# A fused attention and feed-forward kernel: the last head group gets its own tables, and GpSimd takes over the weight split and two row copies

## What is computed

```python
def attn(x, w_attn, w_proj, adapter_wte, gating):        # x is (2, 1024, 512), 32 heads of 16
    q, k, v = split(x @ w_attn.T)                        # q and k then get a rotary embedding
    y = softmax(causal(q @ k.T / sqrt(16))) @ v          # per head
    y = y + gating * softmax(q @ ak.T / sqrt(512)) @ av  # 10 adapter rows, no mask
    return y @ w_proj.T

def ffn(x, base_w, base_b, A, B, router_w):              # 16 experts of rank 64, top 2
    combine = top2(softmax(x @ router_w.T))
    return x @ base_w.T + base_b + 0.5 * einsum(combine, x @ A.T, B)

x = layernorm(x + attn(x, ...))
x = layernorm(x + ffn(x, ...))
```

## Time and profile before

| | us |
|---|---|
| median of three runs | 926.55 |
| lowest and highest of them | 924.72, 932.81 |
| time of the profiled execution | 920.5 |
| its span, first to last instruction | 918.8 |
| PE busy in it | 872.9 (95%) |
| DVE, ACT, POOL busy | 727.6, 471.5, 233.6 |

### The profile page before, as it was taken

One profiled execution on the slowest core, in us unless ns is written; L12 is line 12 of the kernel. 1 busy time (PEld: TensorE's weight loads), 2 busy tenths in 40 slices (PEclk: granted clock), 3 DMA queues, 4 the chain that ended last, 5 costly groups with the idle time before them and its releaser, 6 DMA issues.

```text
span 918.8 us, 15954 instructions
## 1 busy us (share of the span) xinstructions
PE 872.9 (95%) x5420; PEld 565.5 (62%) x5420; DVE 727.6 (79%) x2224; ACT 471.5 (51%) x1036; POOL 233.6 (25%) x269
## 2 busy tenths in 40 slices
PE   5999999988999999999999999999989999999995
PEld 4778787664444444444444444443468888888884
DVE  4675757776889999999999999996477777777766
ACT  4232323111488888888888888887651221212110
POOL 0212121201223332333333323234242222121211
PEclk9999999996599999999999999999999999999999
DMA  7225253604532233333322233333010010101010
GB/s 258 92 69 161 70 161 93 165 18 120 115 60 53 43 61 70 72 71 71 72 48 51 48 70 72 71 102 106 11 36 24 24 46 23 46 23 46 24 36 34
DMA packets 31825, 65.03 MB, mean 71 GB/s; under 512 B 5580, under 2 KB 7052, under 8 KB 31756
## 3 DMA queue, kind: packets, MB, share of 16 engines
q1 hardware_dynamic: 31244, 62.58, 26.3%
q10 hardware_dynamic: 512, 1.57, 0.9%
HBM read 42.54 MB, written 20.97 MB: 69 GB/s over the span
## 4 chain that ended last, share of the span: by engine, by line
PE 81%; DVE 12%; ACT 3%; issue 2%; POOL 1%; DMA 1%; SPq 0%; DVEq 0%; ACTq 0%; POOLq 0%
PE bank L1372 16%; PE bank L1273 16%; PE bank L1283 12%; PE bank L351 10%; PE bank L353 10%; PE bank L352 10%; PE bank L1473 3%; PE bank L1354 2%; DVE xl L814 1%; DVE xtl L1000 1%; ACT xth L757 1%; DVE asb L874 1%; DVE asum L877 1%; ACT asb L640 1%; DVE asum L872 1%
## 5 line engine op out<-in xcount | busy, mean ns | idle before, releaser
L732 ACT ACTIVATE pt<-bank 128x512 f32<-128x512 f32 (+3 forms) x768 | 325.2, 495 | 71.9 <-PE bank L1273 65.5
L896 DVE CUSTOM_DVE_ANT_0 bank<-bank,cmask 128x512 f32<-128x512 f32 (+3 forms) x512 | 234.4, 527 | 12.1 <-PE bank L1283 9.1
L1273 PE MATMUL bank<-qs,ks 50*128 50x512 f32 (+3 forms) x768 | 221.8, 404 | 1.7 <-ACT pt L732 1.3
L1273 PEld LDWEIGHTS bank<-qs,ks 50*128 50x128 f32 x768 | 113.1, 189 | 141.5 <-ACT pt L732 124.4
L1283 PE MATMUL bank<-ks,qs 48*128 48x512 f32 (+3 forms) x768 | 172.3, 402 | 9.0 <-DVE mx L896 6.0
L899 DVE TENSOR_REDUCE mx<-bank 128x1 f32<-128x512 f32 x256 | 161.1, 688 | 14.8 <-PE bank L1283 13.0
L1372 PE MATMUL bank<-pt,vb 128*32 128x512 f32 (+3 forms) x1536 | 167.2, 508 | 0.7 <-POOL pt L570 0.7
L570 POOL TENSOR_SCALAR_AFFINE_SELECT pt<-pt 128x512 f32<-128x512 f32 x128 | 83.4, 651 | 290.3 <-ACT pt L732 290.3
L1283 PEld LDWEIGHTS bank<-ks,qs 48*128 48x128 f32 x768 | 96.0, 194 | 42.8 <-DVE mx L896 16.5
L521 POOL TENSOR_TENSOR part<-rope,part 128x1024 fp32r<-128x1024 f32 x16 | 38.2, 2389 | 190.3 <-ACT part L631 190.3
L757 ACT CAST xth<-bank 128x512 fp32r<-128x512 f32 x16 | 9.4, 586 | 141.4 <-PE bank L1447 141.4
(11 more groups left out here) (149 smaller groups left out, 1405.4 us busy)
## 6 DMA issues: line engine op xcount, KB each, us to landing
q_parts<-part SPq DMA_DIRECT2D x32, 256.0 KB, 3.0
k_parts<-part SPq DMA_DIRECT2D x32, 256.0 KB, 3.2
qs<-q_parts SPq DMA_DIRECT2D x30, 256.0 KB, 4.0
ks<-k_parts SPq DMA_DIRECT2D x30, 256.0 KB, 6.8
vb<-in_x SPq DMA_DIRECT2D x16, 256.0 KB, 2.6
out<-outb SPq DMA_DIRECT2D x16, 256.0 KB, 2.0
qs<-q_parts SPq DMA_DIRECT2D x30, 128.0 KB, 5.0
ks<-k_parts SPq DMA_DIRECT2D x30, 128.0 KB, 5.8
```

The lines of the kernel that those rows point to most:

```text
L732: act.activation(pt[k % PT_BUFS][:, h, 0:width(st)], half(n % SCORE_BUFS)[:, 0:width(st)], ACT.Exp, scale=float(HD) ** -0.5).then_inc(S("e ...
L896: last = ve.tensor_tensor_reduce(blk, blk, cmask[:, BANK - nk * P:], 1.0, NEG, ALU.add, ALU.max, mx[m][:, 0, h, qt:qt + 1])
L1273: pe.matmul(half(n % SCORE_BUFS)[:, 0:q1 - q0], ks[g % 3][r0:r0 + KX, h // 2, kb * P:(kb + 1) * P], qs[g % 3][r0:r0 + KX, h // 2, q0:q1], ...
```

## The change

- Group 15 has tables of its own. Its `weighted` steps are put beside chunks 15, 21, 27, 31, 36, 39, 41, 42, 45, and three after the last chunk; its first half is copied at 32; the transposes go to chunks 13 and 39.
- `t_y(0)` goes from chunk 5 to chunk 0, `t_y(1)` stays at 7. The eight projection pieces go from chunks 11, 12, 15, 16, 21, 24, 25, 29 to 6, 12, 19, 20, 25, 29, 33, 35.
- POOL's two row copies go from the start of group 15 to the start of group 14.
- The projection's weight is loaded in group 11 and split by POOL in group 12, in four pieces of 128x512 (a copy and a subtraction each), ahead of the masks of steps 1 to 3 and after the mask of step 3. DVE has no split(0) any more.
- DVE's order becomes hi_y(0), lo_y(0), hi_y(1), lo_y(1), invert(14, 1), split(1), norms(0, 0), norms(1, 1), invert(15, 0).
- POOL's `normalise(14, 1)` comes after the mask of step 3 in group 15, and `normalise(15, 0)` after all masks of group 15.

```diff
+LAST_VALUES_AT = [15, 21, 27, 31, 36, 39, 41, 42, 45, 48, 49, 50]
+LAST_COPY_AT = [32, 58]
+LAST_NORM_CHUNK = [13, 39]
...
-Y_AT = [5, 7]
-PROJ_AT = [(11, 12, 15, 16), (21, 24, 25, 29)]
+Y_AT = [0, 7]
+PROJ_AT = [(6, 12, 19, 20), (25, 29, 33, 35)]
+SPLIT_GROUP = G - 4
...
+                if g == SPLIT_GROUP - 1:
+                    sp.wait_ge(S("v_built"), GB)
+                    load_weight(0)
                 if g == G - 2:
-                    sp.wait_ge(S("v_built"), GB)
-                    for n in range(2):
-                        load_weight(n)
+                    load_weight(1)
...
+            def split_proj(c_):
+                gp.wait_ge(S("cw0_ld"), 16)
+                gp.tensor_copy(wph[:, c_], wst[0][:, c_]).then_inc(S("wp_high"), 1)
+                gp.wait_ge(S("wp_high"), c_ + 1)
+                gp.tensor_tensor(wpl[:, c_], wst[0][:, c_], wph[:, c_], ALU.subtract).then_inc(S("wp_low"), 1)
             def gp_group(g):
-                if g == G - 1:
+                if g == G - 2:
                     tile_y(0)
                     tile_y(1)
                 for st in range(NS):
+                    if g == SPLIT_GROUP and 1 <= st <= CC:
+                        split_proj(st - 1)
                     if st in DIAGONAL:
...
-                    if HG * (st - 1) < NORM_CHUNK[1] <= HG * st:
+                    if HG * (st - 1) < norm_chunk(g)[1] <= HG * st and g < G - 1:
                         normalise(g, 0)
+                if g == G - 1:
+                    normalise(g, 0)
...
-            split(0)
             hi_y(0, 0)
             lo_y(0, 0)
             hi_y(1, 1)
             lo_y(1, 1)
-            ve.wait_ge(S("cweight_low"), 1)
+            invert(G - 2, 1)
+            ve.wait_ge(S("score_full"), (G - 1) * SCORE_BANKS)
+            split(1)
             norms(0, 0)
-            invert(G - 2, 1)
             norms(1, 1)
             invert(G - 1, 0)
-            ve.wait_ge(S("score_full"), (G - 1) * SCORE_BANKS)
-            split(1)
...
-                    pe.wait_ge(S("cweight_low"), 1)
+                    pe.wait_ge(S("wp_low"), CC)
```

More of the change, by code:

```diff
@@ L104, with values_at, copy_at, norm_chunk @@
 assert COPY_AT[1] - SCORE_BANKS + SCORE_BUFS <= VALUES_AT[0] and COPY_AT[0] < SCORE_BANKS <= COPY_AT[1]
+LAST_VALUES_AT = [15, 21, 27, 31, 36, 39, 41, 42, 45, 48, 49, 50]
+LAST_COPY_AT = [32, 58]
+LAST_NORM_CHUNK = [13, 39]
+def values_at(g):
+    return LAST_VALUES_AT if g == G - 1 else VALUES_AT
+def copy_at(g):
+    return LAST_COPY_AT if g == G - 1 else COPY_AT
+def norm_chunk(g):
+    return LAST_NORM_CHUNK if g == G - 1 else NORM_CHUNK
 SLOTS = NMX + 3
@@ L573, in gp_group @@
                         build_v(g + 1)
-                    if HG * (st - 1) < NORM_CHUNK[0] <= HG * st and g > 0:
+                    if HG * (st - 1) < norm_chunk(g)[0] <= HG * st and g > 0:
                         normalise(g - 1, 1)
-                    if HG * (st - 1) < NORM_CHUNK[1] <= HG * st:
+                    if HG * (st - 1) < norm_chunk(g)[1] <= HG * st and g < G - 1:
                         normalise(g, 0)
+                if g == G - 1:
+                    normalise(g, 0)
             for g in range(G):
@@ L716, in act_group @@
                     st, h = divmod(c, HG)
-                    if c in NORM_CHUNK:
-                        back, i = NORM_OF[NORM_CHUNK.index(c)]
+                    if c in norm_chunk(g):
+                        back, i = NORM_OF[norm_chunk(g).index(c)]
                         if g + back >= 0:
@@ L721, in act_group @@
                     n, k = g * SCORE_BANKS + c, NS * g + st
-                    if c == COPY_AT[0]:
+                    if c == copy_at(g)[0]:
                         evac_y(g, 0)
@@ L981, in split @@
                 ve.tensor_copy(WEIGHTS[n][0], wst[n]).then_inc(S("cweight_high"), 1)
-                ve.wait_ge(S("cweight_high"), n + 1)
+                ve.wait_ge(S("cweight_high"), 1)
                 ve.tensor_tensor(WEIGHTS[n][1], wst[n], WEIGHTS[n][0], ALU.subtract).then_inc(S("cweight_low"), 1)
@@ L1378, in pe_group @@
                     for slot in range(FIRST[c], FIRST[c + 1]):
-                        if not held(g, slot):
+                        if not held(g, slot) or g == G - 1:
                             continue
@@ L1388, in pe_group @@
                             max_scores(g + n, w, use_of(g, slot))
+                    if g == G - 1 and c in norm_chunk(g):
+                        back, i = NORM_OF[norm_chunk(g).index(c)]
+                        trans_out(g + back, i)
                     if g == G - 1:
@@ L1391, in pe_group @@
                     score(g, c)
[L1392 to L1395, removed]
+                    if g > 0 and c + SCORE_BANKS in values_at(g - 1):
+                        weighted(g - 1, values_at(g - 1).index(c + SCORE_BANKS))
+                    if c in values_at(g):
+                        weighted(g, values_at(g).index(c))
             for w in range(EARLY[1], NMX):
@@ L1436, in _ @@
             for st in range(NS):
-                if VALUES_AT[st] >= SCORE_BANKS:
+                if values_at(G - 1)[st] >= SCORE_BANKS:
                     weighted(G - 1, st)
@@ L1483, in base @@
                     pe.wait_ge(S("out_copied"), len(NORM) * G)
-                pe.wait_ge(S("cweight_low"), 2)
+                pe.wait_ge(S("cweight_low"), 1)
                 for c_ in range(CC):
```

## The result

The kernel after takes 916.83 us (median of 20 executions, 913.69 to 923.56), the kernel before 926.46 us (20 executions, 918.85 to 940.33). The ratio is 0.9917, with a 95% interval of 0.9895 to 0.9938: 7.7 us less, with an interval of 5.7 to 9.7. The ratio leaves out executions over 1.5% above the fastest of their kernel, such as those of the kernel before from 933 to 940 us, so it gives less than the medians, which are 9.6 us apart. The forecast was 4.6 us.

What follows compares the result with a forecast made beforehand. PE was taken as the queue to watch, with 5.9 of group 15's 38.0 us waits and slow clock. Terms -1.3 - 1.7 - 0.7 - 1.5 - 0.1 + 0.1 + 0.4 + 0.2 = -4.6 us gave 921.9 us, range 918 to 927.

Steps and rivals of the forecast that it cites:

- t_y(0) at chunk 0: Start of group 15: the first transpose moved earlier removes PE's wait before t_y(1), for -1.3 us.
- The balance: End of group 15: new tables stop PE following ACT, -1.5 us, and make the last mask early, -0.7 us.
- half of it: Rival: gap and clock's fall go, tables only move waits, POOL delays cost 0.7 us: -2.3 us, 924.2; chance 0.18.
- the reckoning by the number of runs alone: Group 15's tables: by the rule on tiling-mode drains alone, they are worth one run of scores, 0.2 us.
- The piece at 25: Group 15: the projection piece at chunk 25 waits for DVE's sum, behind split(1): +0.1 us, up to 0.7.
- POOL in group 14: Start of group 14: row copies ahead of the masks make weighted step 0 late: +0.4 us, bounds 0 to 0.6.
- POOL in group 12: Group 12: three weight pieces among the masks make mask 3 late for weighted step 3: +0.2 us.
- The rival of late pieces: Group 12: slow POOL subtractions leave PE idle 6 us and the clock falls: +2.9 us, 929.5; chance 0.06.
- The fall of the clock: Group 15, around the gap before t_y(1): PE's fall to 1.2 GHz goes with the gap, -1.7 us.
- the clock falls all the same: Rival: a gap at chunk 13 of group 14 or 25 of group 15 brings 1.2 GHz back: -2.9 us, 923.6; chance 0.12.

Runs made afterwards that it cites:

- the later ratio: The kernel after, unchanged, timed again in 12 executions against the kernel before: ratio 0.9944 (0.9915 to 0.9973), median 918.92 us.

## Why the prediction was right in kind and short in size

The way and the place were right; the size was not. The forecast for the median was 921.9 us, in 918 to 927; 916.83 was measured, 1.2 us below the range, though the ratio on the 926.55 us of the forecast gives 918.9. The signs that it named came: no wait before the second transpose, a granted clock of 1.00 in both groups, and the attention ahead of group 15 as long as before (396.3 and 396.4 us); group 15 took 31.95 us, just under the 32 to 34. Point by point, on groups 14 and 15 in executions without a fall of the clock, 62.3 before and 58.3 after:

- **t_y(0) at chunk 0, forecast -1.3.** Measured -2.3 with its pieces (60.57 to 58.30). The gap was priced right, 1.34. The prediction said of the score that waits for ACT "at most its 0.59 is gained there; I count nothing", and that was the wrong choice: 0.54 is gained. The pieces at 6 and 12 leave chunks 10 and 11 together, which gains 0.4; the prediction had one run fewer for all tables, at -0.2, and took half of it away again for wide scores pairing less well.
- **The balance, forecast -0.7 - 1.5.** Measured -2.24. The total is right, and partly by luck, since the 1.5 was picked between 0 and 2.2. The mask's share is smaller than told: putting the old places back adds 0.27 us to its wait, and 0.21 are left in the kernel after, since ACT is still making its last five exponentials in a row when PE's scores end. The rest is 2.0 us, where 1.5 was taken. This also puts out the rival "half of it", and the reckoning by the number of runs alone, 0.2 us.
- **The piece at 25, forecast +0.1.** Nothing. DVE's sum ends at 651.13 and the piece starts at 651.51:

```profile
650.46 0.67 DVE L1046 TENSOR_TENSOR vb<-vb,bank 128x512 f32<-128x512 f32 x1
```
```profile
651.51 0.50 PE L374 MATMUL bank<-wph,qs 128*128 128x512 f32 x1
```

  The conflict of the earlier trace rows took place, POOL's multiplication took 2.65 us, but it was POOL that waited most, and nothing waited for POOL. DVE's subtraction beside it took 2.59 us, where subtractions of 128x2048 with POOL idle take 2.28 to 2.29 in the same trace (L844, L1022): 0.3 us lost on DVE, and the piece still did not wait.
- **POOL in group 14, forecast +0.4.** Measured +0.51 at the step and +0.58 by moving the copies away. The bound of 0.5 from the earlier trace rows was the value; PE gave nothing back.
- **POOL in group 12, forecast +0.2.** Nothing: 26.07 us against 26.09. The piece takes 1.98 us, as priced, but POOL goes from one operation to the next faster than the sum allowed: 7.5 us from the end of the mask of step 0 to that of step 3, three pieces and three masks, instead of 7.9. The rival of late pieces is out: the subtractions took 1.27 to 1.29 us.
- **The fall of the clock, forecast -1.7.** This is the term that was mis-sized. It was taken from one execution as if it belonged to the kernel. In four profiled executions of the kernel before it cost 0, 1.6, 1.6 and 11.4 us (62.3, 63.9, 63.9, 73.7). Without it the forecast's terms for groups 14 and 15 come to -3.1 us, where the executions without a fall show -4.0. What the measured 7.7 us (5.2 by the later ratio) have beyond 4.0 I put down to this term. The mean of the four costs, 3.6 us, is of that size, but four executions are too few to show it, and the executions differ in other stages too. The sign was right. The rival "the clock falls all the same" did not come: no fall is in group 14 or 15 in any of the seven traces without the gap, not even in group 14 behind POOL's 0.51 us.

"Which lies 6 us above the profiled execution for no reason in the trace" was the clause to stop at. A part of the reason stood in another execution's trace.

The Trainium skill, "TensorE: Matmul & The Clock Gate", "Why this matters for your kernels", warns of idle gaps between bursts of matmuls, which let the clock fall. The gaps that it names are longer than this one. In the traces a fall came within 1.3 us of the end of a gap of 1.34 us in three executions of six that have it, and in none of the seven without it.

What stays open: whether the fall needs the old places of the weighted steps as well, and why. All three falls are in the kernel before. With the gap put back and the new places, none of 10 executions was above 927.14 us, and the one that was profiled has no fall; a short one, of 1.6 us, could hide in the others. With both, a half had times above 930 us. That these six had their fall in group 15 is inferred from the one such trace of the kernel before; the profile of this variant is of an execution without one. The intervals of the first ratio of the kernel after, 0.9917, and of the later one, 0.9944, overlap.

## What to carry to other kernels

Put a block whose result another engine must turn around (transpose, cast, subtract) where the queue would wait anyway, and its follower several blocks later; then spread what is left so that PE and ACT run out of work at the same time. An in-order engine that gets a long wait at its head delays everything behind it: put the copy behind the masks that are ready. Before a short wait is priced at its length, read the traces of more than one execution, since what the clock does behind it can cost eight times as much (11.4 us for 1.34), and only in some of them.

## What the runs showed of the hardware

- A wait of PE of 1.34 us, in a stretch of scores of 50 rows, was followed by 0, 3.4 or 27.3 us at 1.2 GHz in the same program. PE was busy throughout the 27.3 us by the profile, and yet got back to 2.4 GHz only at their end.
- Every trace has a stretch at 1.2 GHz of 30.7 to 51.2 us around the start of the attention, beginning at 219 to 224 us, and some have a second of 10.2 us behind it. Groups 0 to 11 last from 316.4 us (with the 30.7) to 323.5 (with the 51.2), whatever the kernel.
- GpSimd casts 128x512 from SBUF to SBUF in 0.61 us and subtracts in 1.28 beside DVE's row maxima, which read PSUM; L589's sum of that size takes 1.28 at its fastest. Beside DVE's subtraction of two SBUF tiles, its 0.62 us multiplication took 2.65. DVE's subtraction of 128x2048 took 2.59 to 2.61 there, when it started while GpSimd was in a mask, and 2.28 to 2.29 with GpSimd idle.
